# Token routing in two parts instead of four: lane one-hots on VectorE and ScalarE instead of GpSimd

## The reference

```python
x = x + moe(lora(x, language_ids))      # layer 0
x = x + ffn(cond(x, prompt_type_ids))   # layer 1

# lora: A, Bm, emb are picked by the batch's language (4 languages, rank 16)
t = einsum('bsd,brd->bsr', x, A);  out = einsum('bsr,bdr->bsd', t, Bm) + emb

# moe: 8 experts, top 2 of the scores, softmax over the two
dot = einsum('bsh,eh->bse', x, expert_embeddings)
weights = softmax(top-2 of dot, others masked)
# an expert takes the first 512 tokens (in token order) that chose it
cap_ones = where(cumsum(weights > 0, axis=0) <= 512, 1, 0)
# relu MLP 512 -> 1024 -> 512 on the tokens of each expert, times weight, added back to their rows
```

## Time and profile before

| | us |
|---|---|
| Median of 3 runs | 885.37 (883.66 to 886.49) |
| The profiled execution, its own time | 881.29 |
| Its span, first to last instruction | 879.5 |
| Busy: TensorE | 768.5 (87%) |
| Busy: VectorE | 532.7 (61%) |
| Busy: ScalarE | 490.1 (56%) |
| Busy: GpSimd | 339.6 (39%) |

### The profile page before, as it was taken

One profiled execution on the slowest core, in us unless ns is written; L12 is line 12 of the kernel. 1 busy time (PEld: TensorE's weight loads), 2 busy tenths in 40 slices (PEclk: granted clock), 3 DMA queues, 4 the chain that ended last, 5 costly groups with the idle time before them and its releaser, 6 DMA issues. The chain is left out here.

```text
span 879.5 us, 10973 instructions
## 1 busy us (share of the span) xinstructions
PE 768.5 (87%) x3828; PEld 495.0 (56%) x3828; DVE 532.7 (61%) x1029; ACT 490.1 (56%) x682; POOL 339.6 (39%) x330
## 2 busy tenths in 40 slices
PE   5774799998999999634999999975799999999997
PEld 3321277776777777412777777764355555555553
DVE  2672445454455455214465565543799999999995
ACT  1110226664377778414566556632687777777783
POOL 0486413243142122204444444420254555444553
PEclk9987789999999999856999999987899999999999
DMA  6999427897295486331111102000012221222212
GB/s 203 347 414 334 146 107 273 288 318 239 97 257 130 131 229 145 43 131 48 49 49 49 40 19 88 1 1 10 27 49 72 73 69 64 68 65 73 72 62 82
DMA packets 42534, 109.07 MB, mean 124 GB/s; under 512 B 4208, under 2 KB 4992, under 8 KB 39280
## 3 DMA queue, kind: packets, MB, share of 16 engines
q1 hardware_dynamic: 35616, 94.71, 30.4%
q0 software_dynamic: 6352, 13.06, 8.0%
q10 hardware_dynamic: 512, 0.61, 0.2%
HBM read 88.63 MB, written 28.13 MB: 133 GB/s over the span
## 5 line engine op out<-in xcount | busy, mean ns | idle before, releaser
L1297 PE MATMUL ps<-ff_q,qt 128*128 128x512 bf16 x512 | 123.8, 387 | 7.1 <-DVE h L1362 6.3
L1323 PE MATMUL ps<-ff_q,ht 128*128 128x512 bf16 x512 | 115.7, 379 | 2.4 <-DVE ht L1379 2.4
L824 PE MATMUL ps<-w_h,inner_l 128*128 128x512 f32 x256 | 102.8, 401 | 3.6 <-DVE inner_l L773 3.6
L1283 POOL TENSOR_SCALAR hb<-h 128x2048 bf16<-128x2048 int8 x32 | 60.8, 1900 | 111.2 <-ACT h L1341 111.2
L639 POOL DMA_INDIRECT x_after_experts<-y,row_of_slot x32 | 51.4, 1605 | 134.7 <-DVE y L759 127.4
L826 PE MATMUL ps<-w_h,inner_h 128*128 128x512 f32 x256 | 101.2, 395 | 0.0
L825 PE MATMUL ps<-w_l,inner_h 128*128 128x512 f32 x256 | 101.1, 395 | 0.0
L1341 ACT ACTIVATE h<-h,to_q 128x2048 int8<-128x2048 f32 x32 | 64.1, 2002 | 44.3 <-DVE to_q L1393 44.3
L1362 DVE SCALAR_TENSOR_TENSOR h<-ps,scale,bias 128x1024 f32<-128x1024 f32 x64 | 81.6, 1279 | 9.3 <-PE ps L1297 9.3
L773 DVE SCALAR_TENSOR_TENSOR inner_l<-ps,inner_h 128x512 fp32r<-128x512 f32 x64 | 44.2, 691 | 69.9 <-ACT inner_h L708 69.4
L1297 PEld LDWEIGHTS ps<-ff_q,qt 128*128 128x128 bf16 x512 | 49.4, 99 | 64.0 <-DVE h L1362 7.5
(11 more groups left out here) (211 smaller groups left out, 1516.1 us busy)
## 6 DMA issues: line engine op xcount, KB each, us to landing
w_in_sb<-in_w_in_t SPq DMA_DIRECT2D x8, 2048.0 KB, 12.7
w_raw<-in_w_out_t SPq DMA_DIRECT2D x16, 1024.0 KB, 5.5
raw<-in_ff_t SPq DMA_DIRECT2D x16, 1024.0 KB, 7.6
xt<-in_x_t SPq DMA_DIRECT2D x8, 1024.0 KB, 9.3
x_after_experts<-in_x SPq DMA_DIRECT2D x8, 1024.0 KB, 16.8
x_sum<-x_after_experts SPq DMA_DIRECT2D x8, 1024.0 KB, 4.8
x<-x_after_experts SPq DMA_DIRECT2D x32, 256.0 KB, 2.7
out<-res SPq DMA_DIRECT2D x32, 256.0 KB, 2.0
```

Source lines behind the costliest of these rows:

```text
L824: pe.matmul(ps[:, s, :], inner_l[:, k % 2, c], w_h[:, k % RING, :], start=k == 0, stop=False)
L1297: m = pe.matmul(ps[:, f, :], qt[:, t, k, :], ff1_q[:, k, f * 512:(f + 1) * 512], start=k == 0, stop=k == KD - 1)
L1323: m = pe.matmul(ps[:, OUT[t3 % 2], :], ht[:, k, :], ff2_q[:, k, :], start=k == 0, stop=k == KF - 1)
```

## The change

- The routing is done in two parts of four batches (`PARTS`) instead of four quarters of two. Every operation of `choose` and `give_slots` is twice as wide and there are half as many. The feature store is made twice with 832 KB instead of four times with 416 KB.
- TensorE, VectorE and ScalarE lists are reordered: one batch after another, each turned behind the product of the next.
- The lane one-hots leave GpSimd. Those of the first choices are made by VectorE (16 `is_equal` per part). Those of the second choices are made by ScalarE: 16 Abs of (lane id - own lane) with a bias per partition, then one Relu of (1 - that) over all 2048 columns.
- The score bias is added by ScalarE when it copies the product out of PSUM, as a bias per partition (score columns are partitions there). `scores` on VectorE goes. The score columns are kept in `feat`, so the language columns move from 68 to 76 (`EMBED` = 72).
- The table of constants is loaded in two pieces: 66 columns that the first masks need, and the rest with a semaphore of its own (`more_consts`). lora_a_t moves from ScalarE's queue to SyncE's. The part `not_first_tile` (64 columns), which nothing read, goes.
- `lane_hot`, `tile_hot` and the new `lane_off` use the memory of the later feed-forward weights.

The diff, cut to its core:

```diff
@@ SyncE
+                    sp.dma_start(lora_b_raw[:], ...).then_inc(consts_in, DMA)
                     sp.dma_start(router_sb[:], ...).then_inc(consts_in, DMA)
-                    sp.dma_start(lora_b_raw[:], ...).then_inc(consts_in, DMA)
                     sp.dma_start(embed_raw[:], ...).then_inc(consts_in, DMA)
+                    sp.dma_start(lora_a_t_sb[:], ...).then_inc(consts_in, DMA)
@@ GpSimd
-                    for q in range(QUARTERS):
+                    for q in range(PARTS):
                         ts = slice(q * QT, (q + 1) * QT)
-                        pool.wait_ge(slot_ready, q + 1)
-                        if q >= 2:
-                            pool.wait_ge(found, q - 1)
-                        lo = slot_lo[:, q % 2, :, :].rearrange("p k t -> p (k t)")
-                        for i in range(PAIRS):
-                            hot = pool.tensor_scalar(lane_hot[:, q % 2, i, :], lane_id_b[:], lo[:, i:i + 1], None, ALU.is_equal)
-                            if i % 4 == 3:
-                                hot.then_inc(lanes_hot, 1)
-                        pool.wait_ge(feat_cp, 2 * (q + 1))
+                        pool.wait_ge(feat_cp, PB * (q + 1))
                         pool.wait_ge(placed, q + 1)
                         pool.dma_start(feat_v[:, ts, :], feat[:, ts, :]).then_inc(feat_out, DMA)
@@ ScalarE
+                    act.dma_start(const[:, 0:FIRST_CONSTS], table[:, 0:FIRST_CONSTS]).then_inc(consts_in, DMA)
                     act.dma_start(lang_i[:], lang.partition_broadcast(P)).then_inc(consts_in, DMA)
-                    act.dma_start(const[:], table).then_inc(consts_in, DMA)
                     act.dma_start(lora_a_sb[:].rearrange("r p k -> r (p k)"), lora_a).then_inc(consts_in, DMA)
-                    act.dma_start(lora_a_t_sb[:], ...).then_inc(consts_in, DMA)
+                    act.dma_start(const[:, FIRST_CONSTS:], table[:, FIRST_CONSTS:]).then_inc(more_consts, DMA)
...
-                        act.activation(feat_t[:, b % 2, :], ps[0:W, FEAT_T_BANK[b % 2], :], ACT.Copy).then_inc(feat_t_cp, 1)
+                        if b == 0:
+                            act.wait_ge(small_cp, 3)
+                        act.activation(feat_t[:, b % 2, :], ps[0:W, FEAT_T_BANK[b % 2], :], ACT.Identity,
+                                       bias=score_bias[:, b:b + 1]).then_inc(feat_t_cp, 1)
...
-                        act.wait_ge(dot_ready, b + 1)
+                        act.wait_ge(feat_tr, b + 1)
...
+                    def hot_lanes(q):
+                        act.wait_ge(slot_ready, q + 1)
+                        if q >= 1:
+                            act.wait_ge(lanes_hot2, q)
+                        for t in range(QT):
+                            last = act.activation(lane_off[:, t, :], lane_id_b[:], ACT.Abs, bias=minus_lo[:, t:t + 1])
+                        last.then_inc(lane_off_ready, 1)
+                        act.wait_ge(lane_off_ready, q + 1)
+                        act.activation(lane_hot[:, q % 2, QT:, :], lane_off, ACT.Relu, bias=1.0, scale=-1.0).then_inc(lanes_hot2, 1)
...
+                    for b in range(BATCH):
+                        keep_feat_t(b)
+                        if b >= 1:
+                            keep_feats(b - 1)
+                        if b == PB:
+                            exps(0)
+                    keep_feats(BATCH - 1)
+                    hot_lanes(0)
+                    high_g(0, 0)
+                    exps(1)
+                    high_g(0, 1)
+                    hot_lanes(1)
+                    high_g(1, 0)
+                    high_g(1, 1)
@@ TensorE
-                    pe.matmul(ps[:, COUNT_BANK, 0:BATCH * EXPERTS], ones[0:LANGS, :],
-                              embed_score[:].rearrange("l b e -> l (b e)"), start=True, stop=True).then_inc(small_mm, 1)
+                    pe.matmul(ps[0:W, COUNT_BANK, 0:BATCH], embed_score[:], lang_row[0:LANGS, :], start=True, stop=True).then_inc(small_mm, 1)
...
+                    for b in range(BATCH):
+                        feats(b)
+                        if b >= 1:
+                            turn_feats(b - 1)
+                        if b == PB + 1:
+                            count(0)
+                    turn_feats(BATCH - 1)
+                    find(0)
                     pe.wait_ge(lora_b_ready, 4)
                     pe.wait_ge(feat_t_cp, BATCH)
                     expand(0, 0)
-                    find(QUARTERS - 2)
                     expand(0, 1)
-                    count(QUARTERS - 1)
+                    count(1)
                     expand(1, 0)
-                    find(QUARTERS - 1)
                     expand(1, 1)
+                    find(1)
@@ VectorE
+                    ve.tensor_copy(score_bias[:], ps[0:W, COUNT_BANK, 0:BATCH]).then_inc(small_cp, 1)
+                    ve.wait_ge(more_consts, DMA)
...
-                        scores(2 * q)
-                        scores(2 * q + 1)
-                        ve.wait_ge(dot_ready, 2 * q + 2)
+                        ve.wait_ge(feat_cp, PB * (q + 1))
...
+                        ve.tensor_scalar(minus_lo[:], lo[:, 1, :], -1.0, None, ALU.mult).then_inc(slot_ready, 1)
...
                         last.then_inc(tiles_hot, 1)
+                        for t in range(QT):
+                            hot = ve.tensor_scalar(lane_hot[:, q % 2, t, :], lane_id_b[:], lo[:, 0, t:t + 1], None, ALU.is_equal)
+                            if t % 4 == 3:
+                                hot.then_inc(lanes_hot, 1)
```

More of the change, by code:

```diff
@@ L34 @@
 EMBED_LOW = 96
+EMBED = LR + EXPERTS
 STACK_1 = EMBED_LOW + LANGS
@@ L53, in constant_table @@
     parts = {
+        "rank_lang": p // RANK,
+        "row": p,
+        "lang_of_lr": spread((np.arange(LR) // RANK)[None]),
         "rank_weight": spread(EXPERTS - e),
@@ L56, in constant_table @@
         "slot_limit": spread((e + 1) * CAP),
-        "not_first_tile": spread(np.tile(np.arange(2 * TPB) > 0, EXPERTS)[None]),
         "slot_id": slots * P + p + 1,
@@ L63, in constant_table @@
         "token_base": p * TILES,
-        "lang_of_lr": spread((np.arange(LR) // RANK)[None]),
-        "row": p,
-        "rank_lang": p // RANK,
         "up_to": p <= np.arange(P)[None],
@@ L218, in _ @@
                 def _(sp):
+                    sp.dma_start(lora_b_raw[:], lora_b_t.rearrange("(p k) r -> p k r", k=KD)).then_inc(consts_in, DMA)
                     sp.dma_start(router_sb[:], router_t.rearrange("(p k) e -> p k e", k=KD)).then_inc(consts_in, DMA)
-                    sp.dma_start(lora_b_raw[:], lora_b_t.rearrange("(p k) r -> p k r", k=KD)).then_inc(consts_in, DMA)
                     sp.dma_start(embed_raw[:], embed_t.rearrange("(p k) r -> p k r", k=KD)).then_inc(consts_in, DMA)
+                    sp.dma_start(lora_a_t_sb[:], lora_a_t.rearrange("(p k) r -> p k r", k=KD)).then_inc(consts_in, DMA)
                     def load_x(b):
@@ L310, in high_g @@
                         act.activation(g_1[0:STACK_1, e, c], ps[0:STACK_1, bank, :], ACT.Copy).then_inc(g_h_cp, 1)
-                    for q in range(QUARTERS):
-                        keep_feat_t(2 * q)
-                        keep_feat_t(2 * q + 1)
-                        keep_feats(2 * q)
-                        keep_feats(2 * q + 1)
-                        exps(q)
-                    for e in range(AHEAD - 1):
-                        for n in (0, 1):
-                            high_g(e, n)
+                    for b in range(BATCH):
[12 more added lines that the diff above has]
+                    high_g(1, 1)
                 @block.tensor
@@ L355, in turn_feats @@
                             pe.wait_ge(feat_cp, b - 1)
+                        if b == 0:
+                            pe.wait_ge(more_consts, DMA)
                         for t in range(TPB):
@@ L370, in find @@
                         for i in range(PAIRS):
[L371 to L372 removed]
+                            if i < QT and i % 4 == 0:
+                                pe.wait_ge(lanes_hot, (q * QT + i) // 4 + 1)
+                            if i == QT:
+                                pe.wait_ge(lanes_hot2, q + 1)
                             m = pe.matmul(ps[:, FIND_BANK, 0:2 * EXPERTS * SB], lane_hot[:, q % 2, i, :],
                                           tile_hot[:, q % 2, i, :, :].rearrange("p a j -> p (a j)"),
[L375 removed]
+                                          start=q == 0 and i == 0, stop=q == PARTS - 1 and i == PAIRS - 1)
                         m.then_inc(found, 1)
@@ L383, in expand @@
                         m.then_inc(g_mm, 1)
-                    for q in range(QUARTERS):
-                        feats(2 * q)
-                        feats(2 * q + 1)
-                        if q >= 2:
-                            find(q - 2)
-                        if q >= 1:
-                            count(q - 1)
-                        turn_feats(2 * q)
-                        turn_feats(2 * q + 1)
```

(15 more changed lines are left out.)

55 lines of the change are left out of this document (26 added, 29 removed).

## The result

The changed kernel took **870.72 us**, median of four runs (869.48 to 870.84), against 884.51 us for the kernel before on the same chip: a ratio of 0.9839 (95% interval 0.9816 to 0.9863), 13.8 us less. The forecast was 872.9 with a range of 866 to 880.5. The profiled execution took 869.48 us, forecast 868.8.

A forecast was written before the change was run, and what follows sets the result against it. The routing block's chain of short operations was taken as the bound, the expert stage following its start. Summed link by link, block end 86.0 for 98.5 gives -12.5 us: 868.8 profiled, 872.9 median, range 866 to 880.5.

The forecast's parts named there:

- The start: Constants loading: two loads open the gate at 6.5 instead of 8.67, worth -2.1 us; VectorE's new wait costs nothing.
- The stall: TensorE idle 35.8 to 37.8 before count(0), at no cost because x for feats(6) comes at 39.6.
- a sign of being wrong: x loads in routing: the forecast is wrong if batches 6 and 7 come before 40 us.
- The links: Part 0's routing chain: choose 5.5 us, give_slots 4.1, VectorE's lanes 2.8, Abs 4.9, Relu 2.0; no table load.
- The tail: Routing from the second exponential, behind high_g(0,0): VectorE ends at 85.2, store lands near 86, block ends 86.0 for 98.5.
- The backlog: x copies queued on the DMA engines at routing's end: gone by about 82, so the last store lands near 86.
- The premise that failed: Expert stage and all behind it move with their start; each microsecond off routing comes off the kernel.
- rival D: Routing's end: late store, and DMA backlog delays expert 0's gathered rows up to 8.4 us; +3.6 us, 889; chance 0.04.
- A: Routing: ScalarE's and VectorE's instructions overlap fully (hot_lanes 5.2 us), x comes in 10.2; -16.5 us, 869; chance 0.14.
- C: Expert stage does not follow: its first weights or x copies end last, gain given back; 885 us; chance 0.05.
- B: Routing's end: part 1's store takes 16.8 us and sets the block end at 93.7; -4.8 us, 880.6; chance 0.12.
- The rule of the Trainium skill: Second choices' lane one-hots: relu-like work belongs on VectorE; using ScalarE leaves some 3 us behind, sign unchanged.

The follow-up runs named there:

- after: The changed kernel itself, with the whole change applied to the kernel before: 870.72 us, ratio 0.9839.
- e1: Changed kernel with the whole constants table again in one load ahead of the gate and lora_a_t last on ScalarE's queue: 874.26 us, ratio 0.9898.
- e2: Changed kernel with part 1's last feature store cut from 832 to 416 KB, the other rows filled early with part 0's features: 873.59 us, ratio 0.9883.
- b1: Kernel before, with only the first choices' lane one-hots moved from GpSimd to VectorE: 873.83 us, ratio 0.9896.
- e5: Changed kernel with all 32 lane one-hots of a part made by VectorE and none by ScalarE: 870.82 us, ratio 0.9823.
- e6: Changed kernel reordered on ScalarE and TensorE so that the second exponential runs ahead of the g evictions: 869.43 us, ratio 0.9849.
- b2: Kernel before, with first choices' lane one-hots on VectorE and constants in two loads, lora_a_t on SyncE's queue: 869.53 us, ratio 0.9816.
- e9: Changed kernel with the second exponential first, four x copies moved to the expert block, and their wait just ahead of the first scatter: 863.88 us, ratio 0.9761.
- e10: Changed kernel with all lane one-hots on VectorE, second exponential first, four x copies late and their wait at the first scatter: 859.82 us, ratio 0.9729.
- e11: Changed kernel, order kept, with four x copies moved to the expert block and their wait just ahead of the first scatter: 868.14 us, ratio 0.9847.
- b3: Kernel before, with first choices' lane one-hots on VectorE, constants in two loads, and four x copies late: 867.73 us, ratio 0.9837.
- e3: Changed kernel with four x copies issued in the expert block, GpSimd's wait for them left ahead of the third gather: 871.24 us, ratio 0.9864.

## Why the prediction was right

**The start.** The gate opened at 5.17, earlier than the forecast's 6.5 and than its lower bound of 6.0. That gained nothing, since x then ended last (1.99 us of waiting): feats(0) at 11.01 for 11.1. VectorE's new wait cost nothing, as costed.

**The stall, mis-sized at nothing.** The sum had TensorE idle at no cost, because x for feats(6) would come at 39.6. x landed after 10.9 us instead of 12.1 and was there at 38.0, before the 40 that the prediction had named as a sign of being wrong; so the stall ended in a batch that took 5.34 for 3.60: about 1.7 us on the path. The text had this case ("if x came early, it would cost 2 us") and took the other. feats(7) still ended at 47.1 (43.49 + 3.60), since the x that came 1.6 us early paid for the slow batch. That is luck.

**The links.** choose of part 0 5.6 for 5.5; give_slots 4.0 for 4.1; VectorE's 16 lanes 2.69 for 2.8; Abs 4.76 for 4.9; Relu 1.91 for 2.0; hot_lanes(0) done at 55.38 for 55.7. No table load joined them (all from its timeline). The wide operations scale from their narrow rows as forecast: differ 1.22 us, tile one-hots 0.49 and 1.29.

**The tail.** The exponential stands behind high_g(0,0) as forecast (VectorE's wait 9.88 for about 11). expand(0,0) ended at about 61.1 for 62.5; from there all is 1.4 to 2.2 us early, VectorE's end 82.97 for 85.2. The store, issued 2.1 us early (74.82 for 76.9), took 10.2 for 9.1 and ended last, at 85.0 for 86; from its landing to TensorE's start passed 1.1 us that the sum did not have. Barrier 86.15 for 86.0, rows turned 94.66 for 94.7. The store's issue came 2.1 us early, its landing and that step took 1.1 us each more: that they cancel to 0.2 us is luck, that the store ends last is not.

**The backlog, misread.** The prediction reasoned from SyncE's last issue that "its backlog is gone by about 82". The last copy landed at 88.0, and in the kernel before at 90.0, 7.5 us behind SyncE's last issue there (82.47). The store's 9.1 us rested on this and on no row of a store of its size; that it came near the measured 10.2 is luck as well.

**The premise that failed**, though not in this sum: "a microsecond taken from the routing block comes off the kernel". It does so only as far as the DMA backlog lets it. In the kernels with all copies in the block whose barrier fell at 86 or later (after, e1, e2, b1), rows were turned 8.5 to 10.1 us behind it; where it fell at 80.93, 81.93 and 83.94 (e5, e6, b2), they were turned 15.3, 12.5 and 12.8 us behind it, at 94.4 to 96.7. With half the copies late the distance was 8.8 to 10.2 us wherever the barrier fell: rows at 87.7 and 87.8 in e9 and e10, 93.1 and 93.2 in e11 and b3, 96.2 in e3. In after itself the gathers were not slowed (3.9 us for the fourth, 4.1 in the kernel before), although the last copy landed 1.9 us behind the barrier. So rival D's mechanism, given 0.04, did not decide here, but an earlier barrier meets it: e5, e6 and b2 do. That it is the backlog and not something else is shown by e9, which differs from e6 in the copies and their wait alone: 863.88 for 869.43.

**The other rivals.** A had x early, which came, but its main term did not: the two lane steps of ScalarE took 6.7 us together (48.67 to 55.38) for its 5.2. Its terms (1.8, 1.1 and 1.5) also add up to -16.9 and not to the -16.5 it names. C did not come: rows were turned 8.5 us behind the barrier and TensorE is full from 107 on. B said that a store of twice the bytes takes longer. Half the bytes took nearly the same (e2, 9.7 for 10.2): the landing time is that of the backlog ahead. The store did end last, 2 us behind VectorE; the forecast had it 0.8 us behind.

**The parts.** The prediction costed the change as one sum and did not say which parts pay. The runs do: VectorE's half of the lane one-hots (b1, 9 us) and the two loads (b1 to b2 4.3 us by medians and 7.1 by ratios, e1 to after 3.5 and 5.2). Parts of four batches, the new order, ScalarE's half and the bias on ScalarE together bring nothing measurable (b2 and after; b3 and e11). None of them was tried alone.

**The rule of the Trainium skill.** The prediction put "relu-like work belongs on VectorE" (ScalarE: Activation LUTs, "Rules for kernel authors") at some 3 us. In e5 row_of_slot came 5.7 us earlier, so on the routing chain the trace agrees and by more; the time stayed (870.82), hidden by the backlog. Where it could show, in e10 against e9, VectorE ended 2.9 us earlier and the barrier fell 1.1 earlier, but the products behind it took 10.04 us for 8.78 and the rows were turned at the same time. TensorE's granted clock in the 4 us before the barrier was 0.50 in e10, where it had waited 8.62 us, and 1.00 in e9, where it had waited 3.29.

## What to carry to other kernels

When a block that ends in a barrier gets shorter, look at what the DMA engines still have queued there: a store, the gathers and the first loads behind the barrier wait for that backlog, and nothing gained on the compute engines beyond it shows. Move bulk copies that nobody needs yet behind the urgent loads, and move the wait for them down to their first user, past every gather queued on the same engine. Split a change that does five things before praising it: here two small edits carried all of it that could be measured.

## What the runs showed of the hardware

- **A store's landing under a full DMA load hardly depends on its size.** Issued between 70 and 81 us with the copies under way, 416 KB took 8.4, 8.6, 9.2 and 9.7 us, 832 KB 8.7 to 11.2. With half the x copies moved behind, 416 KB took 2.7 us (issued at 75.3), and 832 KB 7.7, 7.5, 5.8 and 3.7 us (issued at 69.0, 69.2, 74.7 and 77.9): the later, the less of the remaining copies was in front.
- **A short stall costs TensorE more than its length.** After a stall of 2.84 us a batch of eight products took 5.34 us for 3.60; in e1 6.55. The clock was still at its upper level (2.4 GHz, 1.00) during the stall; the mean of 0.68 over the batch behind it says that it ran partly at the lower (1.2 GHz, 0.50, as between 82.00 and 86.10).
- **A DMA queue's last issue is not the end of its work.** SyncE issued the last copy of x at 69.39 and it landed 18.6 us later.
- **Small VectorE operations are cheap per piece.** 16 one-hots of 128x128 took 2.69 us on VectorE, 0.17 us each, 0.30 us each on ScalarE (4.76 for 16), and 0.63 us each on GpSimd.
- **Two executions of the same code differ by up to 3 us in their rows.** The gate, the same for both, opened at 8.67 in the profile of before and at 9.39 in b1; with the same code on its chain VectorE ended at 85.66 in e3 and 82.95 in e11. From the first turning of rows to the end the thirteen profiled executions took 772 to 777 us. A single profile does not settle a difference of that size.
